# Row maxima in seven tiles of mixed query columns, softmax sums over pairs of key tiles added on GpSimd, and new places for all units of a cross-attention kernel

## The reference

```
qh = proj(layernorm(x), Wq, bq)          # 16 batches, 16 heads, 224 queries, 32 channels
kh = proj(ctx, Wk, bk); vh = proj(ctx, Wv, bv)          # 750 keys
scores = einsum('bhqd,bhkd->bhqk', qh, kh) / sqrt(32)
attn = softmax(scores, axis=-1)
out = einsum('bhqk,bhkd->bhqd', attn, vh)
x = x + concat(out) @ Wo.T + bo
```

## Time and profile before

| | |
|---|---|
| median of 3 runs | 2343.65 us (2338.21 to 2351.19) |
| profiled execution | 2341.8 us, its span 2339.8 us |
| PE busy | 2206.3 us (94%) |
| DVE busy | 1802.4 us (77%) |
| ACT busy | 845.3 us |
| POOL busy | 199.9 us |

### The profile page before, as it was taken

How to read it: one execution, slowest core, us unless ns; L and a number is a source line. 1 busy time by engine, 2 the same in 40 slices (tenths; PEclk the granted TensorE clock), 3 DMA queues, 4 the chain that set the end, 5 groups by cost and what they waited for, 6 DMA issues and landing times. The chain is left out here.

```text
span 2339.8 us, 50409 instructions
## 1 busy us (share of the span) xinstructions
PE 2206.3 (94%) x17444; PEld 1866.8 (80%) x17444; DVE 1802.4 (77%) x3107; ACT 845.3 (36%) x1677; POOL 199.9 (9%) x226
## 2 busy tenths in 40 slices
PE   5999999999999999999999999975999999999998
PEld 4888788887888888888888788853788888888886
DVE  5767777777677776777767777747999999999986
ACT  4544444454444444444445444433111111111111
POOL 1110111110101101111110110100000000000000
PEclk9999999999999999999999999987999999999999
DMA  5343434434344344343443434325010100100100
GB/s 161 100 119 87 120 84 118 121 81 125 94 108 123 80 124 111 91 116 88 114 121 90 120 85 119 88 75 159 17 38 27 38 29 27 40 27 27 36 18 27
DMA packets 124001, 197.38 MB, mean 84 GB/s; under 512 B 29776, under 2 KB 72272, under 8 KB 121280
## 3 DMA queue, kind: packets, MB, share of 16 engines
q1 hardware_dynamic: 123840, 194.86, 30.0%
HBM read 75.67 MB, written 23.33 MB: 42 GB/s over the span
## 5 line engine op out<-in xcount | busy, mean ns | idle before, releaser
L611 DVE TENSOR_REDUCE row_max<-max_bank 112x1 f32<-112x376 f32 (+1 forms) x1024 | 523.0, 541 | 347.8 <-PE max_bank L470 342.8
L536 ACT ACTIVATE probs<-score_bank 125x448 f32<-125x448 f32 x768 | 404.7, 543 | 319.5 <-PE score_bank L485 311.7
L470 PE MATMUL max_bank<-k_high,q_masked 128*112 128x376 f32 (+1 forms) x1024 | 313.0, 353 | 17.1 <-DVE row_max L611 12.8
L485 PE MATMUL score_bank<-qstack,kstack 100*128 100x224 f32 x1536 | 301.7, 281 | 27.6 <-issue 23.7
L485 PEld LDWEIGHTS score_bank<-qstack,kstack 100*128 100x128 f32 x1536 | 262.6, 190 | 59.6 <-issue 51.6
L1145 ACT ACTIVATE f_act_gate<-gate_bank 128x512 f32<-128x512 f32 (+1 forms) x84 | 47.3, 563 | 516.4 <-PE up_bank L1100 516.4
L500 PE MATMUL pv_bank<-probs,values 125*32 125x224 f32 x3072 | 225.1, 366 | 9.2 <-ACT probs L536 9.2
L1100 PE MATMUL gate_bank<-ffn_gate_hi,f_xqt 128*128 128x512 f32 (+1 forms) x672 | 218.9, 387 | 8.1 <-DVE f_xqt L1206 8.1
L444 PE MATMUL proj_bank<-wv_hi,ctx_hi 128*128 128x256 f32 x768 | 221.2, 288 | 4.3 <-DVE wo_lo L690 4.3
L506 PE MATMUL pv_bank<-probs,ones 125*32 125x224 f32 x3072 | 219.4, 358 | 0.0
L444 PE MATMUL proj_bank<-wv_hi,ctx_lo 128*128 128x256 f32 x768 | 216.6, 282 | 0.0
(11 more groups left out here) (121 smaller groups left out, 4166.1 us busy)
## 6 DMA issues: line engine op xcount, KB each, us to landing
kstack<-k_high SPq DMA_DIRECT2D x512, 93.8 KB, 2.2
ctx_raw<-in_ctx SPq DMA_DIRECT2D x16, 1500.0 KB, 6.9
kstack<-k_low SPq DMA_DIRECT2D x256, 93.8 KB, 2.2
qstack<-q_part SPq DMA_DIRECT2D x768, 28.0 KB, 1.9
ffn_quant<-fw_share SPq DMA_DIRECT2D x48, 176.0 KB, 1.9
fw_raw<-ffn_quant SPq DMA_DIRECT2D x33, 256.0 KB, 4.1
xn<-in_x SPq DMA_DIRECT2D x16, 448.0 KB, 7.9
res<-in_x SPq DMA_DIRECT2D x16, 448.0 KB, 4.0
```

Of the source, the lines that this page charges most:

```text
L470: nc.tensor.matmul(out[0:QH, 0:hi - lo], q_masked[t % 2][:, j, half * QH:(half + 1) * QH], k_part[t % 2][0][:, lo:hi], start=True, stop=Tr ...
L485: last = nc.tensor.matmul(score_bank[j % 2][:, k * SQ:(k + 1) * SQ], kstack[t % 2][0:STK, j, kt * KW:kt * KW + P], qstack[t % 2][:, j, :], ...
L536: nc.scalar.activation(probs[p][:, j, :, :], score_bank[j % 2][0:KW, 0:2 * SQ].rearrange("p (k q) -> p k q", k=2), ACT.Exp, scale=float(DK ...
L611: nc.vector.tensor_reduce(row_max[:, half, j, kh:kh + 1], mbank[0:QH, 0:KSPLIT[kh + 1] - KSPLIT[kh]], AX.X, ALU.max).then_inc(max_reduced, 1)
```

## The change

Three things are changed.

1. **Maxima.** The 4 x 224 = 896 masked query columns of a group are cut into `MT` = 7 tiles of 128 columns, whichever heads they belong to. There are 14 max units of 128 columns instead of 16 of 112, one join and one transpose in place of two. The transposed result has seven rows, one per tile. DVE, not ACT, spreads it over `qstack`: multiplied by a block of the identity, so that row m holds its values only in the columns of tile m and zeros elsewhere. `kstack` has seven rows of ones, and the score matmul contracts over 103 rows.
2. **Sums.** New `pair` units on GpSimd add the two key tiles of a `probs` tile into `pair_sum`, and new `sum` units on PE multiply these with the ones: three blocks for each slot instead of six. The exponential of the next slot into a `probs` tile waits for the pair too.
3. **Places.** Every number of the table is new, and all three `pv` units can stand in the next slot now (a place of 12 or more).

The core of the diff:

```diff
+MT = HG * SQ // P
+STK = SHIFT + MT
-        "max": (0.15, 0.15, 0.74, 1.46, 1.97, 2.82, 3.42, 4.78, 4.89, 5.54, 6.68, 6.73, 7.87, 7.94, 8.54, 9.17),
-        "shift": (5.97, 10.64),
+        "max": (0.05, 0.05, 0.5, 0.67, 1.09, 1.26, 2.4, 3.77, 4.18, 6.66, 7.16, 7.75, 8.33, 8.62),
+        "shift": 11.01,
...
+def attend_units(g):
+    at = PLACES[g % NG]
+    return [(place, (kind, g, p)) for kind, places in (("pair", "pair"), ("pv", "pv"), ("sum", "pv")) for p, place in enumerate(at[places])]
...
+    placed += [(place, unit) for place, unit in attend_units(g) if place < 12]
+    if not (first and g == 0):
+        placed += [(place - 12, unit) for place, unit in attend_units(g - 1) if place >= 12]
...
# PE
-                    nc.tensor.matmul(out[0:QH, 0:hi - lo], q_masked[t % 2][:, j, half * QH:(half + 1) * QH],
+                    nc.tensor.matmul(out[:, 0:hi - lo], masked_columns[t % 2][:, m * P:(m + 1) * P],
-                    nc.tensor.transpose(out[:, 0:QH], neg_max[:, u[2], :],
-                                        ident[0:QH, 0:QH]).then_inc(made["shift"], 1)
+                    nc.tensor.transpose(out[:, 0:P], neg_max[:, :], ident[:, :]).then_inc(made["shift"], 1)
-                        for j in range(HG):
-                            last = nc.tensor.matmul(pv_bank[t % 2][j * DK:(j + 1) * DK, SQ:2 * SQ], ones[0:KW, :],
-                                                    probs[p][:, j, k, :], start=False, stop=(kt == KT - 1),
+                elif kind == "sum":
+                    p = u[2]
+                    reached(pe, paired, count(b, *u))
+                    for j in range(HG):
+                        last = nc.tensor.matmul(pv_bank[t % 2][j * DK:(j + 1) * DK, SQ:2 * SQ], ones[0:KW, :],
+                                                pair_sum[p][:, j, :], start=False, stop=(p == 2),
# ACT
                     if j == 0:
                         reached(act, made["pv"], count(b, "pv", t - 1, p))
+                        reached(act, paired, count(b, "sum", t - 1, p))
-                elif kind == "shift":
-                    act.wait_ge(made["shift"], count(b, *u))
-                    row = mbank[SHIFT:STK, 0:QH].unsqueeze(1).to_broadcast([HG, HG, QH])
-                    nc.scalar.activation(qstack[t % 2][SHIFT:STK, :, u[2] * QH:(u[2] + 1) * QH], row,
-                                         ACT.Copy).then_inc(shift_copied, 1)
# DVE
+                elif kind == "shift":
+                    dve.wait_ge(made["shift"], count(b, *u))
+                    reached(dve, made["score"], count(b, "score", t - 2, 2, 3))
+                    nc.vector.tensor_tensor(shift_rows[t % 2][SHIFT:STK, :, :],
+                                            mbank[SHIFT:STK, 0:P].unsqueeze(1).to_broadcast([MT, MT, P]),
+                                            ident[SHIFT:STK, SHIFT:STK].unsqueeze(2).to_broadcast([MT, MT, P]),
+                                            ALU.mult).then_inc(shift_copied, 1)
# POOL
+                if kind == "pair":
+                    p = u[2]
+                    pool.wait_ge(exp_done, count(b, "score", t, p, HG - 1))
+                    reached(pool, made["sum"], count(b, "sum", t - 1, p))
+                    nc.gpsimd.tensor_tensor(pair_sum[p][:, :, :], probs[p][:, :, 0, :],
+                                            probs[p][:, :, 1, :], ALU.add).then_inc(paired, 1)
```

More of the change, by code:

```diff
@@ L55 @@
 FFN_SLOTS = (0, 1, 3)
[L58 to L66, removed]
@@ L91 @@
         "load": 2.6,
         "load_res": 6.6,
[L93 to L116 removed]
+        "add_bias": 11.9,
@@ new lines @@
+        "ffn_quant": (1.82, 4.09, 4.67, 4.8, 4.86, 5.37, 7.12, 9.92, 10.16, 11.5, 11.55),
+        "ffn_store": 11.9,
+    },
+    {
+        "max": (0.05, 0.39, 0.51, 0.54, 1.41, 2.73, 4.14, 4.51, 4.86, 6.4, 9.06, 9.25, 9.54, 10.5),
+        "shift": 11.9,
+        "pv": (12.09, 13.92, 14.94),
+        "pair": (5.8, 9.61, 11.28),
+        "inverse": (2.55, 3.18),
+        "heads": 5.32,
+        "heads_hi": 5.95,
+        "sum_lo": 11.9,
+        "k": (1.3, 4.76),
+        "k_lo": (2.86, 5.76),
+        "q": 7.77,
+        "q_lo": 9.26,
+        "v": (9.34, 11.03, 11.9),
+        "out": (3.59, 6.28),
+        "ctx": (8.12, 8.76, 10.82, 11.73),
+        "xt": (1.21, 4.74),
+        "xt_lo": (11.9, 11.9),
+        "norm": (1.54, 5.67),
+        "norm2": (5.88, 7.73),
@@ new lines @@
+        "ffn_quant": (0.81, 4.69, 4.73, 4.75, 5.0, 8.58, 9.01, 11.39, 11.88, 11.89, 11.9),
+        "ffn_store": 9.18,
+    },
+    {
+        "max": (0.05, 0.05, 0.28, 0.29, 1.59, 2.56, 4.03, 5.5, 5.95, 6.12, 6.94, 8.07, 8.92, 11.21),
+        "shift": 11.9,
+        "pv": (8.06, 12.76, 14.03),
+        "pair": (0.09, 4.44, 7.78),
+        "inverse": (4.05, 6.89),
+        "heads": 8.32,
+        "heads_hi": 9.66,
+        "sum_lo": 11.9,
+        "k": (5.12, 5.92),
+        "k_lo": (5.91, 6.66),
+        "q": 6.27,
+        "q_lo": 7.0,
+        "v": (9.45, 11.72, 11.9),
+        "out": (3.86, 10.91),
+        "ctx": (0.3, 0.53, 1.75, 2.55),
+        "xt": (0.81, 3.86),
+        "xt_lo": (1.41, 5.17),
+        "norm": (2.74, 5.6),
+        "norm2": (6.08, 6.55),
@@ new lines @@
+        "ffn_quant": (4.84, 7.48, 9.07, 10.79, 11.9, 11.9, 11.9, 11.9, 11.9, 11.9, 11.9),
+        "ffn_store": 2.18,
+    },
+    {
+        "max": (0.05, 0.05, 0.35, 0.43, 0.76, 0.79, 2.49, 3.24, 3.97, 4.96, 5.49, 7.35, 8.51, 9.64),
+        "shift": 11.9,
+        "pv": (10.94, 12.41, 13.07),
+        "pair": (0.05, 2.73, 7.38),
+        "inverse": (3.58, 6.31),
+        "heads": 8.5,
+        "heads_hi": 8.13,
+        "sum_lo": 11.63,
+        "k": (0.05, 3.53),
+        "k_lo": (3.78, 5.47),
+        "q": 5.25,
+        "q_lo": 9.57,
+        "v": (8.92, 11.09, 11.9),
+        "out": (5.77, 9.51),
+        "ctx": (2.83, 3.46, 5.47, 8.95),
+        "xt": (1.92, 11.9),
+        "xt_lo": (3.89, 4.98),
+        "norm": (4.06, 6.48),
+        "norm2": (3.93, 6.71),
@@ L313, in attention @@
     pv_bank = [bank(f"pv_bank{i}") for i in range(2)]
-    names = ("score", "max", "shift", "k", "q", "v", "xt", "out", "pv")
+    names = ("score", "max", "shift", "k", "q", "v", "xt", "out", "pv", "sum")
     made = {n: sem(f"{n}_made") for n in names}
@@ L359, in index_of @@
             return ((b + unit[1]) * 2 + unit[2]) * KT + unit[3]
-        per = {"score": 12, "max": 16, "shift": 2, "k": 2, "q": 1, "pv": 3, "sum": 1}
+        per = {"score": 12, "max": 2 * MT, "shift": 1, "k": 2, "q": 1, "pv": 3, "sum": 3, "normalized": 1}
         if kind in per:
@@ L440, in body @@
                     half, kt = u[2], u[3]
+                    if half == 0 and kt == 0:
+                        reached(pe, lo_done["ctx"], count(b, "ctx", t, KC - 1))
                     n = 0
```

178 lines of the change are left out of this document (65 added, 113 removed).

## The result

The changed kernel takes 2416.28 us (median of 4 runs, 2415.62 to 2417.22) against 2347.42 us (2338.21 to 2354.36) for the kernel before on the same chip: a ratio of 1.031, interval 1.028 to 1.033. Forecast were 2263 us, in a range of 2230 to 2318. The sign was wrong, and the time is that of the second rival (the chain at the slot's end), which had 6%.

What follows compares the result with a forecast made beforehand. PE's matmul stream was taken to bound the attention. Per batch -6.3 (matmuls removed) + 1.0 (DVE delays) + 0.3 (slot-end shift) = -5.0 us, -80 us over 16 batches, giving 2263 us; range 2230 to 2318.

Steps and rivals of the forecast that it cites:

- the second rival (the chain at the slot's end): PE's first score of each slot waits behind the spreading, clock falls: +5.7 us per batch, 2435 us; 6%.
- PE's own work: Matmuls removed from PE: sums 1.14, maxima 0.34, transposes 0.1 us per slot; 6.3 us per batch, 101 over 16 batches.
- VectorE's load without pairs: DVE per batch: reductions and joins go, four spreadings come; 69.9 us becomes 69.2, as before.
- The operations' own prices: Durations of the new instructions: 2.0 us for a pair sum on POOL, 1.0 us for a spreading on DVE.
- The hold: POOL operations hold DVE steps with SBUF operands; at today's rate 4.4 us more DVE time per batch, at worst 24.
- How much of that reaches PE: Share of DVE's added 4.4 us that PE waits for: 1.0 us more per batch, range 0 to 4.4.
- The shift at the end of a slot: Chain from last maximum to next score: DVE and PE equal at 3.2 us in slot 1; 0.3 us per batch.
- The pairs' own latency: Wait of PE's sums for the pair sums: costed at nothing, 2 us per slot without cover by other PE units.
- VectorE paces part of the slots: First rival: pairs fall on DVE steps more often, PE feels all 4.4 us; -1.6 us per batch, 2318 us; 16%.

Runs made afterwards that it cites:

- tiny pairs: Changed kernel with each GpSimd pair sum cut to 32 of 896 elements, so softmax sums are wrong: 2235.67 us, ratio 0.953.
- without pairs: Changed kernel without pair sums on GpSimd, six blocks of ones per slot on PE again, new maxima and places kept: 2348.11 us, ratio 1.001.
- sums that nobody reads: Changed kernel with pair sums of 32 elements, each followed by a GpSimd sum of 896 weight elements into an unused tile: 2410.44 us, ratio 1.027.
- the old places: Place table of the kernel before; with it the whole changed code took 2577.02 us, the kernel before with only pair sums added 2499.09 us.
- the last version: Changed kernel with pair sums, masks and bias sums in pieces, quantization steps and a layernorm step moved, everything computed: 2236.02 us, ratio 0.953.
- the new maxima alone: Kernel before with only the maxima part (seven tiles, one transpose, spreading on VectorE), no pair sums, its own places: 2407.13 us, ratio 1.027.

## Why the prediction was wrong

- **PE's own work: right as a sum.** Forecast 6.3 us per batch less. A batch falls from 95.6 to 88.3 us with tiny pairs, 7.3 us. Of the 1.0 beyond the sum 0.7 is the loop's edge, 1.17 us for 1.9; the rest I haven't split. The terms were not measured one by one: without pairs the 28 us of the maxima and transposes do not show.
- **VectorE's load without pairs: right.** 69.2 us forecast; with tiny pairs 234.47 of 300 us busy (stretch 600 to 900), times 88.3 is 69.0.
- **The operations' own prices: right.** 2.16 us for 2.0 and 1.10 for 1.0. The Trainium skill's page "GPSIMD Engine Reference", section "Performance versus the Vector engine", has 4497 ns for 2048 elements, by proportion an estimate of 1.97 us; the trace has 10% more.
- **The hold: half of what it is.** VectorE was busy 237.45 / 300 x 98.9 = 78.3 us per batch, 9.3 more than with tiny pairs, not 4.4. I had taken the rate at which GpSimd's old operations happened to meet VectorE's steps; the pairs return at fixed places of the slot and meet the same steps each time, L871 in more than half of its cases.
- **"How much of that reaches PE": the step that failed.** I took today's wait of 1.1 us per batch and raised it in proportion to the load, to 1.0 us more, with all 4.4 as the ceiling. Measured: 7.0 us more idle time and, by difference, 2.6 of slower clock, more than twice the ceiling. What the runs show in its place: PE waits 109 us for the spreading and 41 for maxima where I had some 30 in all, and this comes back with sums that nobody reads (111 and 44) and goes with tiny ones (25 and 10). An average can't give this: a hold costs what stands behind it, and here that is the first score and so all of PE, at places that return in each batch.
- **"The shift at the end of a slot": failed by omission.** The sum of 3.2 us for VectorE in slot 1 used free durations (three times 0.5), one section after the one in which I had worked out that pairs hold such steps for 2 us. PE stood 2.3 us there where I had 0.3, and 4.75 at the loop's edge, where I had called five steps hidden by the edge's 1.9 and, were they not, put 1 to 1.5 us per batch on them, which I left out of the sum.
- **The pairs' own latency: right at these places,** nothing waits for them. At the old places it is 53 to 58 us.
- **The rivals.** "The chain at the slot's end" had the mechanism, the place and the point from which it decides (1.6 us per slot; measured 4.75 + 2.34 over four slots is 1.8), and the lower clock too. Its "against" was wrong: that the pair starts only after the last exponential, "when only a step or two are left", is when it does the harm (650.66), since one held step lets the next run into the bias sums. "VectorE paces part of the slots" is refuted as a matter of load: in the last version it is 82% busy and PE waits for nothing long.
- The Trainium skill, "SBUF — State Buffer", section "Who interferes with whom", was cited for a VectorE instruction with two SBUF inputs, which blocks fully beside a GpSimd operation that reads SBUF. For such steps the runs agree: 2.31 us for L883 beside the unread sum (0.53 when free), 1.47 us for L873 beside a bias sum. The longest hold of the changed kernel, L871, is on a step with one input (2.16 us beside a 2.11 us sum), so the rule as I quoted it was too narrow for what followed. I let it change the load and not the chain.

What stays open: why the new maxima alone cost 61 us at the old places, where only the waits are known, how much of the last version's gain is each of its five moved numbers, and how the last 50 us before it split between the other pieces and the order.

## What to carry to other kernels

Work that goes to GpSimd is not free for VectorE, even where nothing waits for its result: count the places where a VectorE step with SBUF operands stands before something that PE waits for, and price each at the whole operation, not at an average rate. Cut such an operation into pieces about as long as a VectorE step, though it takes more time in all. Then let the waits say where optional steps go: a rule to keep them out of the chain from join to spreading would have been wrong, since the fastest version has three of them there in slot 3 (2.4 us, hidden behind PE's projections), and 60 us more lay in VectorE's order, partly in waits for DMAs ahead of a reduction.
